# A gated cross-attention and mixture-of-experts block: norms on GpSimd, another order of the prologue, all experts in one sequence, queries in three fp16 passes

## The reference, cut to what matters

```
x = x + tanh(g_xattn) * cross_attention(layernorm(x), ctx)          # 16 heads of 64, 1444 context rows of 96
h = layernorm(x)
xf = h                                                             # the block's residual
q, k, v = rmsnorm(h) @ wq, @ wk, @ wv                              # 16 heads of 8, 100 tokens of one batch
X  = xf + softmax(q k^T / sqrt(8)) v @ wo
h2 = rmsnorm(X)
moe = shared(h2) + sum over the top 2 of 8 experts of weight * swiglu_e(h2)     # d_ff 256
x = x + tanh(g_ffn) * (X + moe)
```

## Time and profile before

| | us |
|---|---|
| three runs | 1434.51, 1433.46, 1437.46 (median 1434.51) |
| the profiled execution | 1439.96 |
| its span, first to last instruction | 1438.1 |
| busy: PE, DVE, ACT, POOL | 1279.4, 1012.1, 819.5, 674.9 |
| mean granted clock of PE | 0.972 of full |

### The profile page before, as it was taken

The page is one execution under the profiler, slowest core; times in us unless marked ns, Lnnn a source line. Parts: engine busy times, 40 slices in busy tenths (PEclk is TensorE's granted clock), DMA queues, the critical chain, the costliest instruction groups (busy, mean ns, idle before and its releaser), DMA issues.

```text
span 1438.1 us, 34393 instructions
## 1 busy us (share of the span) xinstructions
PE 1279.4 (89%) x14216; PEld 924.2 (64%) x14216; DVE 1012.1 (70%) x1825; ACT 819.5 (57%) x1476; POOL 674.9 (47%) x591
## 2 busy tenths in 40 slices
PE   4759999999999999999999989998989897868898
PEld 4236666666666666767676767676767675646676
DVE  2679686868676768685868676767676776836765
ACT  1135666666666566656565656665656564635644
POOL 3024445545455555455444444544545444443454
PEclk9589999999999999999999999999999997989999
DMA  8120302020303020302020221212020200000000
GB/s 222 35 60 13 74 13 74 12 74 13 74 13 74 13 74 13 69 12 72 12 58 24 49 37 33 53 28 58 14 73 13 58 13 14 13 14 1 8 8 11
DMA packets 122273, 57.21 MB, mean 40 GB/s; under 512 B 108262, under 2 KB 117706, under 8 KB 122122
## 3 DMA queue, kind: packets, MB, share of 16 engines
q1 hardware_dynamic: 122122, 55.07, 16.6%
HBM read 15.38 MB, written 0.82 MB: 11 GB/s over the span
## 4 chain that ended last, share of the span: by engine, by line
PE 65%; DVE 15%; ACT 9%; issue 5%; DMA 3%; POOL 2%; SPq 0%; DVEq 0%; ACTq 0%; POOLq 0%
PE psum L763 15%; PE psum L744 8%; PE psum L825 7%; PE psum L745 7%; PE psum L746 7%; DVE p_lo L435 5%; DVE mx L1270 4%; PE psum L778 4%; PE psum L854 3%; PE psum L867 3%; PE psum L817 3%; PE psum L791 3%; PE psum L876 2%; ACT p_hi L972 2%; DVE kbd L1290 2%
## 5 line engine op out<-in xcount | busy, mean ns | idle before, releaser
L435 POOL TENSOR_TENSOR p_lo<-p,p_hi 128x768 f16<-128x768 f32 (+1 forms) x144 | 296.1, 2057 | 466.7 <-ACT p_hi L967 254.0
L1270 DVE TENSOR_REDUCE mx<-psum 128x1 f32<-128x512 f32 (+1 forms) x624 | 378.5, 652 | 68.2 <-PE psum L825 63.8
L966 ACT ACTIVATE p<-psum 128x768 f32<-128x768 f32 (+1 forms) x256 | 214.0, 836 | 283.1 <-PE psum L746 283.0
L763 PEld LDWEIGHTS psum<-c_both,p_hi 128*128 128x128 f16 x4992 | 285.5, 99 | 90.3 <-issue 31.2
L763 PE MATMUL psum<-c_both,p_hi 128*128 128x97 f16 (+1 forms) x4992 | 327.7, 207 | 5.5 <-ACT acc_sb L982 5.3
L435 DVE TENSOR_TENSOR p_lo<-p,p_hi 128x768 f16<-128x768 f32 (+1 forms) x240 | 282.7, 1178 | 30.5 <-ACT p_hi L967 26.9
L744 PE MATMUL psum<-qk_hi,cT_both 97*128 97x384 f16 (+1 forms) x768 | 259.2, 337 | 23.3 <-ACT p_hi L967 12.8
L825 PE MATMUL psum<-cT_both,qk_hi 96*128 96x512 f16 (+1 forms) x624 | 220.2, 383 | 45.7 <-DVE mx L1270 26.9
L745 PE MATMUL psum<-qk_lo,cT_both 96*128 96x384 f16 (+1 forms) x768 | 257.9, 336 | 0.0
L746 PE MATMUL psum<-qk_hi,cT_both 96*128 96x384 f16 (+1 forms) x768 | 255.6, 333 | 0.0
L971 ACT ACTIVATE p<-psum 128x384 f32<-128x384 f32 (+1 forms) x256 | 130.0, 508 | 171.3 <-PE psum L746 171.3
(11 more groups left out here) (190 smaller groups left out, 1940.1 us busy)
## 6 DMA issues: line engine op xcount, KB each, us to landing
c_both<-c_new SPq DMA_DIRECT2D x16, 768.0 KB, 3.9
ctx_nat<-in_ctx_dram SPq DMA_DIRECT2D x16, 528.0 KB
wg<-in_L_ffn_e_gate_dram SPq DMA_DIRECT2D x1, 1024.0 KB, 5.4
wu<-in_L_ffn_e_up_dram SPq DMA_DIRECT2D x1, 1024.0 KB, 7.8
wd<-in_L_ffn_e_down_dram SPq DMA_DIRECT2D x8, 128.0 KB, 5.7
aT<-a_new SPq DMA_TRANSPOSE x64, 2.9
out_dram<-x SPq DMA_DIRECT2D x4, 200.0 KB
x<-in_x_dram SPq DMA_DIRECT2D x1, 600.0 KB
```

Of the source, the lines that this page charges most:

```text
L435: engine.tensor_tensor(p_lo[0:m, i % 3, 0:w], p32[0:m, i % 3, 0:w], p_hi[0:m, i % 3, 0:w], ALU.subtract).then_inc(lo_made(b, i)[0], 1)
L763: t = mm(psum[:, ACCB + bank, k * (C + 1):k * (C + 1) + wide], p[0:m, i % 3, n * P:(n + 1) * P], c[parity][0:m, j, 0:wide], start=(j == 0 ...
L966: a(to32, src, ACT.Exp, scale=DH ** -0.5)
L1270: v.tensor_reduce(mx[:, rt, part:part + 1], bank[:, 0:w], AX.X, ALU.max)\
```

## The change

It does five things.

1. **Norms on POOL.** `norm_1` has three instructions on small columns (two sums and one power over two columns) and then writes `hn` and `xf` (100 x 128) on POOL itself. `ln` moves from step 8 to step 7, behind `y1`, and `NORM1_AT` from 8 to 7, which puts `norm_1` ahead of POOL's `p_lo` of step 7. `norm_2` has three small instructions and writes `hn2`. DVE does neither any more. With the planner's costs unchanged, step 7 of a middle batch now has one `p` instead of two and step 8 four instead of three; `f0` moves from the middle of step 9's `pv_unit` to just before it.
2. **Queries in fp16.** `Mh` and the normed x are kept as fp16 halves, and a `q` unit is 12 fp16 matmuls (4 heads by 3 passes) instead of 4 fp32 ones. DVE writes two tiles where it wrote one for each `x` unit.
3. **Prologue.** The x of batches 0 to 3 is loaded first, with a semaphore of its own, the context of batch 0 right behind w_q and w_k, and the expert weights only after `row_of(0)`, that is at the end of body 0. POOL clears `c_new` before other tiles. `p` units give way to 13 units `w`: three matmuls into three neighbouring banks and one reduction over 1444 columns, two sets of banks in turn. `ctx_lo(1)` comes ahead of `token_rstd(1)`, and `ctx_made(1, 1)` ahead of `send_row(0)`.
4. **Experts in one sequence.** All 72 units `e` stand in `LAST`, with the self attention of batch 15 and its router hung in at fixed units (`CHAIN`). The lag of `down` is 4. Units e 0 to e 3 run before `y1`.
5. **Last normalise on DVE.** The last accumulator is divided on DVE with a reciprocal instead of POOL's power.

```diff
-    plan[8].append(("ln", 0))
-    plan[9].append(("xf", 0))
+    plan[7].append(("ln", 0))
+    plan[7].append(("xf", 0))
-    CTX_AT, NORM1_AT, ACC0_AT, NORM2_AT = 0, 8, 14, 22
+    CTX_AT, NORM1_AT, ACC0_AT, NORM2_AT = 0, 7, 14, 22
...
-    PREP = [("q", n) for n in range(4)] + \
-           [("p", n) for n in range(NPU)] + [("m", 0)]
+    PREP = [("q", 0), ("q", 1)] + [("w", n) for n in range(3)] + [("q", 2)] + \
+           [("w", n) for n in range(3, 6)] + [("q", 3)] + [("w", n) for n in range(6, RT)] + [("m", 0)]
+    NE = 4 * EU
+    CHAIN = {3: ["y1"], 4: ["ln"], 6: ["xf", 0], 7: [1], 8: [2, 3, 4, 5], 10: [6, 7], 11: [8, 9], 12: [10, 11], 13: [12, 13],
+             14: [14], 15: [15], 16: ["rs"], 18: ["h2", 16], 19: ["r"]}
+    CHAIN.update({22 + 2 * n: [("ru", n)] for n in range(RT_UNITS)})
...
+    for m in range(NE + LAG + 2):
+        LAST.append(("e", m))
+        for u in CHAIN.get(m, []):
+            LAST.append(u if isinstance(u, tuple) else ("f", u) if isinstance(u, int) else (u, 1 if u == "r" else 0))
...
+            load(x1[:, 0:4, :], x[0:4].rearrange("b s d -> s b d"), x0_in)
             load(wq_nat, w_q, wqk_in)
             load(wk_nat[:, :], w_k, wqk_in)
-            load(x1[:, 0:4, :], x[0:4].rearrange("b s d -> s b d"), x_in)
+            load_ctx(0)
...
             ctx_made(0, 0)
-            send_row(0, 0, len(PREP) - 1)
             ctx_made(1, 1)
+            send_row(0, 0, AT_FIRST - 1)
             turn(0, 0)
             row_of(0, "first", 0)
+            load_experts()
...
             def norm_1(c):
-                small(c, "var+eps", g.tensor_scalar(pcol("var+eps"), var, LN_EPS, None, ALU.add))
-                small(c, "rstd", g.tensor_tensor(pcol("rstd"), pcol("var+eps"), half, ALU.pow))
-                small(c, "rstd2", g.tensor_tensor(pcol("rstd2"), pcol("rstd"), pcol("rstd"), ALU.mult))
-                small(c, "ms", g.tensor_tensor(pcol("ms"), pcol("rstd2"), var, ALU.mult))
-                small(c, "ms+eps", g.tensor_scalar(pcol("ms+eps"), pcol("ms"), RMS_EPS, None, ALU.add))
-                small(c, "r", g.tensor_tensor(pcol("r"), pcol("ms+eps"), half, ALU.pow))
-                small(c, "rr", g.tensor_tensor(pcol("rr"), pcol("r"), pcol("rstd"), ALU.mult))
+                g.tensor_scalar(pvar[:, 0:1], var, LN_EPS, None, ALU.add).then_inc(pool_step, 1)
+                g.tensor_scalar(pvar[:, 1:2], var, 1.0 + RMS_EPS, LN_EPS * RMS_EPS, ALU.mult, ALU.add).then_inc(pool_step, 1)
+                pool.wait_ge(pool_step, p_at(c, "var+eps2"))
+                small(c, "rr", g.tensor_tensor(prstd, pvar, minus_half[0:S, 0:2], ALU.pow))
+                g.tensor_scalar(hn[:, :], row, aggr[:, 0:1], prstd[:, 1:2], ALU.subtract, ALU.mult).then_inc(pool_step, 1)
+                g.tensor_scalar(xf[:, :], row, aggr[:, 0:1], prstd[:, 0:1], ALU.subtract, ALU.mult).then_inc(pool_step, 1)
...
+                if kind == "w":
+                    if n == 0:
+                        pe.wait_ge(ct_in, 16)
...
+                    for part in range(MP):
+                        cols = slice(part * MW, min(KV, (part + 1) * MW))
+                        t = mm(psum[:, 3 * (n % 2) + part, 0:cols.stop - cols.start], qk_hi[parity][0:C, padded_rows(n)],
+                               cT_hi[parity][0:C, cols], start=True, stop=True)
...
                 if kind == "q":
                     for k in range(4):
-                        t = mm(bank[0:C, k * S:(k + 1) * S], Mh[:, 4 * n + k, :], xlnT[:, tok(b)],
-                               start=True, stop=True)
+                        for w, x_ in ((Mh_hi, xl_hi), (Mh_hi, xl_lo), (Mh_lo, xl_hi)):
+                            t = mm(bank[0:C, k * S:(k + 1) * S], w[:, 4 * n + k, :], x_[:, tok(b)],
+                                   start=(k == 0 and w is Mh_hi and x_ is xl_hi), stop=(k == 3 and w is Mh_lo),
+                                   skip_group_check=True)
```

More of the change, by code:

```diff
@@ L138, in flamingo_kernel @@
     A_LAST = sum(u[0] in KINDS_LAST for u in flat)
-    AT_FIRST = len(PREP)
+    AT_FIRST = sum(u[0] not in NO_BANK for u in PREP)
     AT_LOOP = AT_FIRST + A_FIRST
@@ L184, in flamingo_kernel @@
     NPS = len(P_STEPS)
-    SET_POOL = ["-1/2", "zero ident", "ident", "zero ident16", "ident16", "lnr0", "minus one", "pad p_hi", "pad p_lo", "zero a_new",
-                 "zero c_new", "ones c_new", "ones end", "pad qk_hi0", "pad qk_hi1", "mx", "ones v9", "ones mask", "mask above", "head_mask",
-                "n1"] + [f"rank of {e}" for e in range(E)] + ["rw", "lnr1", "lnr2", "lnr3"]
+    SET_POOL = ["-1/2", "zero ident", "ident", "zero ident16", "ident16", "zero c_new", "ones c_new", "ones end",
+                "pad qk_hi0", "pad qk_hi1", "lnr0", "minus one", "pad p_hi", "pad p_lo", "mx", "ones v9", "ones mask",
+                "mask above", "head_mask", "zero a_new", "n1"] + [f"rank of {e}" for e in range(E)] + \
+               ["lnr1", "lnr2", "lnr3", "rw"]
@@ L436, in probs_rest @@
                                  ALU.subtract).then_inc(lo_made(b, i)[0], 1)
-        Mh_r = Mh[:, :, :].rearrange("p (a r) c -> p r a c", r=2)
+        Mh_hi_r, Mh_lo_r = (t[:, :, :].rearrange("p (a r) c -> p r a c", r=2) for t in (Mh_hi, Mh_lo))
         Nh_hi_r, Nh_lo_r = (t[:, :, :].rearrange("p (a r) c -> p r a c", r=2) for t in (Nh_hi, Nh_lo))
@@ L575, in _ @@
                 step(f"pad qk_hi{q}", g.memset(qk_hi[q][:, ROWS:], 0.0))
+            token_rstd(0)
+            step("minus one", g.memset(minus_one[:, :], -1.0))
+            step("pad p_hi", g.memset(p_hi[:, :, PW:], 1.0))
+            step("pad p_lo", g.memset(p_lo[:, :, PW:], 0.0))
             step("mx", g.memset(mx[:, :, :], 0.0))
@@ L633, in _ @@
+                small(c, "r2", g.tensor_tensor(pms[:, 1:2], pms[:, 0:1], half, ALU.pow))
+                g.tensor_scalar(hn2[:, :], x2[:, c, :], pms[:, 1:2], None, ALU.mult).then_inc(pool_step, 1)
             ctx_lo(0, 0)
+            step("zero a_new", g.memset(a_new[:, :, :, :], 0.0))
             pool.wait_ge(w_in, 16 * W_LOADS)
@@ L682, in _ @@
                     norm_2(B - 1)
-                elif kind == "e" and 0 <= n - 2 < EU:
-                    hidden_lo(0, n - 2)
-            inputs_lo(1)
-            def group(q):
-                for n in range(EU):
-                    hidden_lo(q, n)
-            groups(pool, group)
+                elif kind == "r":
+                    inputs_lo(1)
+                elif kind == "e" and 0 <= n - 1 < NE:
+                    hidden_lo(n - 1)
         @block.tensor
@@ L912, in _ @@
             run_aux(aux, LAST, B, "end", 0)
-            def group(q):
-                for n in range(EU + LAG):
-                    if n < EU:
-                        gate_up(q, n)
-                    if n >= LAG:
-                        down(q, n - LAG)
-            groups(pe, group, lambda: pe.wait_ge(h_lo_out, 2))
         @block.scalar
@@ L1099, in _ @@
             layernorm(0, "c")
+            set_wait(dve, set_pe, SET_PE, "Mh0")
+            for k in range(2):
+                ins = cp(Mh_hi_r[:, 0, 4 * k:4 * k + 4, :], psum[:, k, 0:4 * C].rearrange("p (k c) -> p k c", c=C))
+            step("Mh0hi", ins)
+            for k in range(2):
+                ins = tt(Mh_lo_r[:, 0, 4 * k:4 * k + 4, :], psum[:, k, 0:4 * C].rearrange("p (k c) -> p k c", c=C),
+                         Mh_hi_r[:, 0, 4 * k:4 * k + 4, :], ALU.subtract)
+            step("Mh0", ins)
+            set_wait(dve, set_pe, SET_PE, "xlnT0")
+            step("xhi0", cp(xl_hi[:, 0:GW], psum[:, AUXB + 1, 0:GW]))
+            step("xlnT0", tt(xl_lo[:, 0:GW], psum[:, AUXB + 1, 0:GW], xl_hi[:, 0:GW], ALU.subtract))
             set_wait(dve, set_act, SET_ACT, "tx")
```

340 lines of the change are left out of this document (167 added, 173 removed).

## The result

The changed kernel takes 1400.5 us (median, 1398.2 to 1403.3) beside 1434.0 for the kernel before: a ratio of 0.9757, 95% interval 0.9734 to 0.9780. It is faster, by 33.5 us where 63.5 were forecast, and lies 3.5 us above the range. The spans of the two profiled executions, 1438.1 and 1398.8, differ by 39.3 (the one before is 6 us above its median), and the stages split this difference. Ratios in this document leave out one execution of `e3`, the only one in a slow state (2114.4 us at a mean granted clock of 0.556). The mark between stages is the copy of `mrow`, which comes once per batch.

A forecast was written before the change was run, and what follows sets the result against it. PE, busy for 89% of the span, was taken as the bound. The terms -15 - 8 + 4 - 10.5 - 10 - 4 - 20 = -63.5 us gave 1376.5 from the profiled execution, 1371 off the median; range 1347 to 1397.

The forecast's parts named there:

- Norms: Middle batches: the wait of 1.4 us for hn goes, 0.6 to 0.7 for p_lo comes; -10 us, bounds +8 and -20.
- Rival A: Norms: the new p_lo wait is as long as the old or longer; 0 to +8, 1381 to 1389 us, chance 0.2.
- Queries: q units in 15 bodies: 0.54 us each instead of 0.73, 0.7 us per body; -10.5 us, bounds -3.5 and -12.
- Rival C: Queries: the weight load sets the pace, up to 91 ns; +22 instead of -10.5, 1403 us, chance 0.03.
- Prologue: Up to the first score matmul: earlier context chain and 13 wide reductions; -15 us, bounds -11 and -18.
- Body 0: First body: the 10.5 us wait for the transposed context goes; -8 us, bounds -4 and -10.5; -8.7 with its queries.
- Body 1: Second body: expert loads delay the transposed context of batch 2; +4 us, bounds 0 and +7; +2.6 with queries and norms.
- Last body: Last batch: the hole of 6.8 us shrinks to about 2.8; -4 us, bounds -1 and -5.5.
- End: Last product to last down: experts in one sequence, 145.4 us instead of 165.3; -20 us, bounds -14 and -25.
- rival B: End: batch 15's chain isn't hidden among the experts; the end gives only -13, 1378 us, chance 0.15.

The follow-up runs named there:

- e3: The changed kernel with a fourth fp16 pass (low times low) for the queries, 16 matmuls per unit for 12: ratio 0.9835 to before, profiled execution 1411.2 us.
- e1: The kernel before with the norms part of the change alone: 1449.2 us, ratio 1.0089 to before, middle batch 74.87 us.
- e2: The changed kernel with the norms part put back as before: 1389.9 us, ratio 0.9689 to before, middle batch 72.56 us.
- e6: The changed kernel with only xf moved behind the p_lo of step 7 on POOL: ratio 0.9498 to before, middle batch 71.57 us.
- e9: The changed kernel with the p_lo of step 9 on DVE instead of POOL: ratio 0.9665 to before, middle batch 73.04 us.
- e10: The changed kernel with xf behind step 7's p_lo and the expert loads between body 1's two accumulator transposes: 1359.5 us, ratio 0.9468 to before.
- e12: e10 with the last division of the accumulator back on POOL: 1363.1 us, ratio 0.9497 to before.

## Why the prediction was wrong, and where it was right

**Norms: the step that failed.** Forecast -0.7 us per batch, measured +1.1 to +1.5 (`e1`, and changed against `e2`). The wait for `hn` did go, and one for `p_lo(7)` came, as said. Two terms were wrong.

- The size. `hn` took 0.81 and `xf` 0.79 us, not 0.55: a third of the columns of the row costs two thirds of its time. Part of that is the row itself, which multiplies by one scalar, where `hn` and `xf` take two (a difference and a product). The product of `norm_2`, also 100 x 128 and with one scalar (L628), took 0.62 at its shortest and 0.93 in the median (both lines stand below). The power over two columns was 0.73, as taken. So `p_lo(7)` was 3.1 us behind `aggr`, not 2.6, and PE waited 1.0 for it, not 0.6 to 0.7. That is 0.4 of the error.
- The sentence "Behind `p_lo` on POOL only the next `p_lo` waits, with two steps of room". True of POOL's queue, and the wrong queue to look at. `p_lo(7)` started at 309.50, 4.5 us after ACT had finished its input, beside the one subtraction that DVE had there, and POOL's next was ready by the time it ended. DVE stood for both, 3.90 us in place of 0.95, and with it all that is in DVE's order behind: two maxima, `qT`, `kbd`. PE's wait for `kbd` grew from 0.43 to 1.19 and those for `p_hi` by 0.4 per batch. Rival A had the place ("by the port") but was priced at 0 to +8 us for the 14 batches. Measured, with `e2` as the base, it is +1.49 against -0.7 in each, some 21 us for 14. By name the waits account for 1.1 of the 1.49 (`hn` -1.4, `p_lo` +1.0, `kbd` +0.8, `p_hi` +0.5, `ex` +0.2). The other 0.4 stand in the traces as busy time of PE, 68.35 us against 67.96 per batch over the 13; why is open.

The lines of the first point, shortest, median and longest ns:

```profile
L619 POOL TENSOR_SCALAR hn<-x,aggr,ps x16: 804/805/1317, 160.4 to 1265.2; 100x128 f32<-100x128 f32 x16
L628 POOL TENSOR_SCALAR hn<-x,ps x16: 617/930/931, 204.9 to 1296.2; 100x128 f32<-100x128 f32 x16
```

The prediction named the port and the row of it, POOL's 2.44 in place of 1.64, and read it as POOL being held back by DVE. It didn't ask the reverse: what DVE loses while POOL holds. That row was in the trace of before as well, 7 us ahead of the one it read and in other batches too (2.05 at 242.58, 2.37 at 464.07). POOL's subtraction comes first, then DVE's:

```profile
389.83 1.64 POOL L435 TENSOR_TENSOR p_lo<-p,p_hi 128x768 f16<-128x768 f32 x1 [2.03 <-ACT p_hi L967]
390.24 2.05 DVE L435 TENSOR_TENSOR p_lo<-p,p_hi 128x768 f16<-128x768 f32 x1
```

DVE's ends at 392.29, 0.82 us behind POOL's, and has lost 1.1. The Trainium skill ("SBUF — State Buffer", "Who interferes with whom") has that side too: whoever issues first keeps the shared ports for the whole instruction and the other fully blocks, and a DVE instruction with two inputs in SBUF is among those that meet GpSimd there. The 0.80 to 0.82 us behind POOL's end, in these two rows and in three later kernels, agree with it.

**Queries: right, and low.** A unit took 283.70 to 284.25, that is 0.55 us, or 45.5 ns a matmul; the first and the last row of the twelve and what follows:

```profile
283.70 0.21 PE L826 MATMUL psum<-xl_hi,Mh_hi 128*96 128x100 f16 x1
...
284.20 0.21 PE L826 MATMUL psum<-xl_hi,Mh_lo 128*96 128x100 f16 x1
284.25 0.46 PE L755 MATMUL psum<-c_both,p_hi 128*128 128x96 f16 x7
```

The gain was 1.2 us per batch by `e2`, more than the 0.7, because the waits at the first `p` shrank by 0.4 as well. Rival C (91 ns) is ruled out. The 80 ns that the Trainium skill (TensorE: Matmul & The Clock Gate, the LDWEIGHTS section) gives for these weights don't set the pace here either. Two units of body 0 did take 83 ns a matmul (24 from 53.81 to 55.8), with the granted clock at 0.50, the lower level. The units of the prologue took 83 as well (24 from 22.48), where the profile has a clock of 1.00; that is open.

**Prologue: -13.0 for -15.** The chain (the view of the earlier trace rows) ran through the queries, as said, and not through the context:

```profile
12.18 3.70 PE psum L705 x16
...
16.74 3.67 PE psum L705 x16
...
22.48 1.25 PE psum L826 x12
...
25.10 1.38 PE psum L815 x3
...
37.19 11.10 DVE mx_row L1256 x7
...
51.91 0.50 PE psum L736
```

The halves of `Mh` took 3.7 each, not 3.2, and the first `w` came at 25.1, not 23.5. That is 1.6 of the 2.0 us that are missing. A reduction took 1.59 us (11.10 / 7), as in the forecast (20.5 / 13), and the way from the last reduction to the first score took 3.6.

**Body 0: -8.8 for -8.7.** The wait of 10.5 us for the transposed context is gone, as said. That the number agrees is partly luck: 2.5 us of waits for maxima were to come back, and it is 0.7 (4.7 and 0.3 before, 4.0 and 1.7 now), while PE is busy for 68.8 us where it was 68.4, though the queries were to take 0.7 away. From 67 to 97 us DVE is busy for 29.1 of 30 us, so DVE paces that part of body 0, which stays at 75.4 to 75.9 in `e6`, `e9` and `e10` too. **Body 1: +5.0 for +2.6.** The mechanism was right (4.7 us of wait for the context, forecast 4), and the norms' loss adds to it. Against a middle batch it has no wait for maxima (0.8 us there), and PE is busy for 69.8 us and not 68.1: the granted clock was 0.50 from 146 to 150 us, behind the wait.

**Last body: -2.5 for -4.** The hole of 6.8 fell to 1.5, where 2.8 was forecast, and a wait of 2.5 for the late `p_lo(7)` appeared. In the waits of 1120 to 1240 us:

```profile
PE psum L736 <- ACT p_hi L959: 4.6, 8, 1.7
PE psum L755 <- POOL p_lo L430: 3.5, 2, 2.5
PE psum L871 <- POOL hn L619: 1.5, 1, 1.5
```

**End: -23.1 for -20.** The order of the chain hid behind the experts, as the forecast held against rival B; `gate_up` 2 waited 2.2 us for DVE's division (2.5 forecast). PE is busy for 135.5 of the 142.2 us, 4.9 less than before, where 2.5 were expected from the clock. The row that the 2.5 came from gives more: a mean clock of 0.93 over 58.7 us lacks 7% of them, by my estimate 4.1 us. `e12` suggests that the place of the division matters by 4, in one profile each.

## What to carry to other kernels

- Read the trace for both engines of a shared resource: here the row that shows the loss on DVE stood 7 us ahead of the row that was read.
- An instruction put in front on a queue costs more than its own time if what it delays is an instruction that shares a resource with another engine: look at what the delayed one will then start beside, and at what stands behind its neighbour.
- When several parts of a change meet in one loop, take them apart: the sum here, +0.26 us per batch, looked like "the gain was swallowed by the next wait", and was a gain of 1.2 and a loss of 1.5. A wait whose releaser changes its name from one kernel to the next hasn't grown by that.
- A large load had no good or bad time by itself here, only a good or bad place in its queue. It did best directly behind the last transfer that was wanted soon.

## What the runs showed of the hardware that was not expected

- Two subtractions on POOL in direct succession (1.62 us each) don't let a DVE subtraction that was issued 0.14 us after the first in between: it ran when both were over (3.90 us). When another kind of instruction (`xf`) stood between them, DVE's did come in between, and that one stood for it (1.49 for 0.79). Whether the kind of instruction or the moment of issue decides this, no run here shows. Maxima on DVE, which read PSUM, weren't held: the two behind `p_lo(8)` took 1.27 us in the changed kernel, where POOL was idle, and 1.27 in `e6` (304.99 to 306.26), beside POOL's `xf` and subtraction.
- On POOL an instruction with two scalars takes 0.79 to 0.81 us for 128 columns on 100 partitions. With one scalar it takes 0.62 at its shortest for the same, and 1.26 for 384 columns on 128 partitions. A straight line through the last two leaves some 0.3 us whatever the width, an estimate that takes the number of partitions not to matter.
